# Fusion attention written out: key rows loaded, one maximum and one exponential over 1500 keys

## The reference

```
memory_proj = einsum('bme,de->bmd', memory, W_mem)
scores = einsum('bnd,bmd->bnm', hidden_states, memory_proj) / sqrt(256)
attn = softmax(scores, axis=-1)
memory_context = einsum('bnm,bmd->bnd', attn, memory_proj)
gate = sigmoid(concat([hidden_states, memory_context]) @ W_gate.T + b_gate)
fused = hidden_states + gate * memory_context; return rmsnorm(fused, norm_w)
```

## Time and profile before

| | |
|---|---|
| median of 3 runs | 1597.53 us (1596.61 to 1602.24) |
| the profiled execution | 1597.96 us, its span 1596.2 us |
| PE busy | 1476.0 us, 92% |
| DVE busy | 945.8 us, 59% |
| ACT busy | 621.8 us, 39% |
| POOL busy | 539.6 us, 34% |
| DMA moved | 82.96 MB, mean 52 GB/s |
| the stage in question | about 690.8 to 818.7 us |

### The profile page before, as it was taken

The page is one execution under the profiler, slowest core; times in us unless marked ns, Lnnn a source line. Parts: engine busy times, 40 slices in busy tenths (PEclk is TensorE's granted clock), DMA queues, the critical chain, the costliest instruction groups (busy, mean ns, idle before and its releaser), DMA issues.

```text
span 1596.2 us, 21925 instructions
## 1 busy us (share of the span) xinstructions
PE 1476.0 (92%) x8042; PEld 781.9 (49%) x8043; DVE 945.8 (59%) x1605; ACT 621.8 (39%) x1014; POOL 539.6 (34%) x425
## 2 busy tenths in 40 slices
PE   6779999999999899989988899999999889999898
PEld 3346555555555444446654344455344344555344
DVE  6877666666666264114437677777333768778440
ACT  1253466666666520035542233334122333333131
POOL 1620488888888910000001133332000133333000
PEclk9989999999999999989999999999999989999999
DMA  7001532232331140023212001110031001110000
GB/s 253 0 2 36 136 97 71 76 98 64 84 80 50 27 138 0 0 78 106 88 34 64 0 25 43 40 36 1 2 112 65 0 21 40 36 36 13 2 0 23
DMA packets 42276, 82.96 MB, mean 52 GB/s; under 512 B 6252, under 2 KB 28188, under 8 KB 42156
## 3 DMA queue, kind: packets, MB, share of 16 engines
q1 hardware_dynamic: 42160, 81.48, 17.7%
HBM read 59.31 MB, written 0.97 MB: 38 GB/s over the span
## 4 chain that ended last, share of the span: by engine, by line
PE 79%; DVE 12%; POOL 3%; ACT 2%; issue 2%; DMA 0%; SPq 0%; POOLq 0%; ACTq 0%; DVEq 0%
PE psum L1810 21%; PE psum L2393 8%; PE psum L2051 5%; PE psum L2027 5%; PE psum L2001 3%; PE psum L2334 3%; DVE WBZ L1713 3%; PE psum L1984 3%; PE psum L2201 3%; PE psum L1970 2%; POOL XN L780 2%; PE psum L2365 2%; DVE WA L1453 2%; PE psum L2401 2%; PE psum L2385 2%
## 5 line engine op out<-in xcount | busy, mean ns | idle before, releaser
L1453 DVE TENSOR_REDUCE WA<-psum 112x2 f32<-112x1000 f32 x192 | 229.8, 1201 | 89.9 <-PE psum L2001 89.9
L780 POOL TENSOR_TENSOR XN<-XN,WBZ 125x896 f32<-125x896 f32 x128 | 266.5, 2082 | 16.8 <-POOL XN L780 0.9
L1172 ACT ACTIVATE WA<-psum,y_bias 125x448 f32<-125x448 f32 x192 | 121.1, 633 | 227.7 <-PE psum L2388 226.7
L1006 ACT ACTIVATE WBZ<-psum 125x896 f32<-125x896 f32 x192 | 175.5, 915 | 43.9 <-PE psum L2027 33.3
L2393 PE MATMUL psum<-WA,ctxN 125*128 125x448 f32 x384 | 179.8, 552 | 0.4 <-ACT WA L1172 0.4
L812 POOL TENSOR_TENSOR XN<-const,y_max 112x896 bf16<-112x896 f32 x32 | 53.7, 1679 | 309.6 <-DVE y_max L1700 237.4
L1700 DVE CUSTOM_DVE_ANT_0 XA<-psum,WA 112x375 bf16<-112x375 f32 x240 | 122.7, 540 | 35.9 <-PE psum L2365 35.9
L803 POOL TENSOR_SCALAR ctxT<-ctxT 128x375 f32<-128x375 f32 x32 | 56.1, 1754 | 190.3 <-ACT std L881 187.8
L2027 PE MATMUL psum<-R 100*125 100x224 f16 x768 | 110.6, 266 | 0.0
L1713 DVE RECIPROCAL WBZ<-WBZ 128x224 f32<-128x224 f32 x68 | 105.2, 1549 | 1.2
L2365 PE MATMUL psum<-XB,R 128*112 128x375 f16 x240 | 77.7, 344 | 22.7 <-DVE y_max L1700 22.7
(11 more groups left out here) (266 smaller groups left out, 2567.4 us busy)
## 6 DMA issues: line engine op xcount, KB each, us to landing
R<-WA SPq DMA_DIRECT2D x192, 93.8 KB, 2.2
ctxT<-in_ctxT SPq DMA_DIRECT2D x12, 750.0 KB, 4.2
R<-in_ctxT SPq DMA_DIRECT2D x12, 750.0 KB, 5.4
WA<-in_ctxT SPq DMA_DIRECT2D x8, 750.0 KB, 4.2
ctxT<-in_ctxT SPq DMA_DIRECT2D x32, 187.5 KB
ctxN<-in_ctx SPq DMA_DIRECT2D x32, 187.5 KB
WBZ<-in_x_w SPq DMA_DIRECT2D x4, 1024.0 KB, 6.3
WA<-bias_rows SPq DMA_DIRECT2D x30, 82.0 KB, 3.8
```

What stands on the lines that cost most here:

```text
L780: nc.gpsimd.tensor_tensor(z_sum[b % 2][0:TK, :], first[0:TK, :], z_p[t % 4][0:TK, :], ALU.add)\
L1006: nc.scalar.activation(z_p[t % 4][0:TK, :].rearrange("p (k n) -> p k n", k=2), psum[0:TK, s:s + 2, 0:2 * GC], ACT.Exp, scale=float(CHD0) * ...
L1172: nc.scalar.activation(y_pT[t][0:TK, g * HALF:(g + 1) * HALF], bank[2 + u % 3][0:TK, 0:HALF], ACT.Exp, bias=y_bias[0:TK, bass.ds(b * NT + ...
L1453: V.tensor_reduce(z_mx[0:PR, r:r + 3:2, c], psum[0:PR, lo:lo + 2, 0:PC], AX_X, ALU.max)\
```

## The change

The stage is written out for all eight walks, without loops, and in another way:

- Key rows are loaded from in_ctx, two loads a walk of 125 partitions x 4 pieces of 1536 bytes (750 KB each). PE turns no context, and ACT copies none. Walk 0's rows are loaded with its columns; SP issues the rows of walk i when the values of walk i - 2 are done (m_pv), the columns when the scores of walk i - 2 are (m_scores). Both stand in SP's one list.
- The scores of a walk fill four banks (8 products). One maximum on DVE and one exponential on ACT read all 1500 columns. There is one set of four banks: scores of walk i + 1 wait for the exponential of walk i.
- The 12 probability parts are 125 adjacent columns each, turned four at a time, copied by ACT in three copies of 512 columns, and all 12 value products add up in one bank.
- The quotient is taken by DVE (m_divide) straight from that bank. The queries are read in place from XA, 64 columns each (8 of them belong to the next batch; their results are dropped).
- POOL has no part in the stage.

On SP:

```diff
-            with sp.Fori(0, HB // 2 - 1) as i:
-                for p in range(2):
-                    wait_alone(sp, "x1_scores", CHUNKS * (2 * i + p + 1) + 1)
-                    two_contexts(2 * i + p + 2, p)
+            def m_columns(i):
+                for j in range(2):
+                    b = 2 * i + j
+                    load(m_ctxT[i % 2][j], a["ctxT"][:, b * NK:(b + 1) * NK], f"m_columns{i % 2}")
+            def m_rows(i):
+                for j in range(2):
+                    at = (2 * i + j) * CHUNKS * TK
+                    load(m_ctxN[i % 2][j][0:TK].rearrange("k (c t) x -> k c (t x)", c=CHUNKS),
+                         a["ctx"][at:at + CHUNKS * TK, :].rearrange("(c k) x -> k c x", c=CHUNKS), f"m_rows{i % 2}")
...
+            m_columns(0)
+            m_rows(0)
             emptied(sp, ("down", 1, 1))
+            m_columns(1)
+            m_rows(1)
+            for i in range(2, HB):
+                sp.wait_ge(sem("m_scores"), i - 1)
+                m_columns(i)
+                sp.wait_ge(sem("m_pv"), i - 1)
+                m_rows(i)
+            sp.wait_ge(sem("m_pv"), HB)
```

On ACT (its m_turned copies four turned parts, its m_back the result turned back):

```diff
+            def m_exps(i):
+                act.wait_ge(sem("m_max"), i + 1)
+                if i > 1:
+                    act.wait_ge(sem("m_turned"), PARTS3 * (i - 1))
+                nc.scalar.activation(m_p[i % 2].rearrange("p (c k) -> p c k", c=CHUNKS), m_scores, ACT.Exp,
+                                     bias=nmax_all[:, i % 2:i % 2 + 1], accum_out=lsum_all[:, i % 2:i % 2 + 1])\
+                    .then_inc(sem("m_exp"), 1)
...
+            for i in range(HB):
+                m_turned(i, 0)
+                m_turned(i, 1)
+                if i + 1 < HB:
+                    m_exps(i + 1)
+                m_turned(i, 2)
+                if i > 0:
+                    m_back(i - 1)
```

On DVE:

```diff
+            def m_maximum(i):
+                dve.wait_ge(sem("m_scores"), i + 1)
+                if i > 1:
+                    dve.wait_ge(sem("m_exp"), i - 1)
+                V.tensor_reduce(nmax_all[:, i % 2:i % 2 + 1], m_scores, AX_XY, ALU.max, negate=True)\
+                    .then_inc(sem("m_max"), 1)
```

On PE (m_turned turns four parts of 125 columns, m_attended multiplies them with the key rows, m_back turns the result back):

```diff
+            def m_scored(i):
+                pe.wait_ge(sem(f"m_columns{i % 2}"), 32 * (i // 2 + 1))
+                if i > 0:
+                    pe.wait_ge(sem("m_exp"), i)
+                for u in range(CHUNKS):
+                    for j in range(2):
+                        at = i * PR + j * S
+                        mm = pe.matmul(bank[u][QP * j:QP * (j + 1), 0:CK], m_flat[:, at:at + QP],
+                                       m_ctxT[i % 2][j][:, u * CK:(u + 1) * CK], start=True, stop=True)
+                mm.then_inc(sem("m_scores"), 1)
...
+            m_scored(0)
+            for i in range(HB):
+                if i + 1 < HB:
+                    m_scored(i + 1)
+                m_turned(i, 0)
+                m_turned(i, 1)
+                if i > 0:
+                    m_back(i - 1)
+                m_attended(i, 0)
+                m_turned(i, 2)
+                m_attended(i, 1)
+                m_attended(i, 2)
```

More of the change, by code:

```diff
@@ L60 @@
 NT = NK // TK
+PARTS3 = NT // 4
 QG = 4
@@ L293, in build @@
                       .rearrange("p (b h s) -> p b h s", b=B, h=4) for t in (XB, XN))
-        cmax, nnew, ddec, alpha, rsum = (sb(n, [P, 4]) for n in ("cmax", "nnew", "ddec", "alpha", "rsum"))
+        cmax = sb("cmax", [P, 4])
         QH = HEADS * S
@@ L393, in take @@
             return bank[bk]
-        FOURS = 2 * NT // 4
         LANDED = 16 * 2
[L400 to L403, removed]
         def entry(eng, col, hi, lo=0):
             return eng.value_load(table[0:1, bass.ds(col, 1)], min_val=lo, max_val=hi)
[L408 to L449, removed]
         def ahead(b, t):
@@ L1589, in _, with m_divide @@
                     add_to_x(("down", h, m), m, h)
-            attention("x1", 0, None)
+            def m_maximum(i):
[4 more added lines that the diff above has]
+                    .then_inc(sem("m_max"), 1)
+            def m_divide(i):
+                dve.wait_ge(sem("m_exp"), i + 1)
+                if i > 1:
+                    dve.wait_ge(sem("m_normed"), i - 1)
+                then(V.reciprocal(rl[i % 2][:, 0:1], lsum_all[:, i % 2:i % 2 + 1]))
+                dve.wait_ge(sem("m_pv"), i + 1)
+                if i > 1:
+                    dve.wait_ge(sem("m_back"), i - 1)
+                V.tensor_scalar(m_o[i % 2], bank[6 + i % 2][:, 0:C], rl[i % 2][:, 0:1], None, ALU.mult)\
+                    .then_inc(sem("m_normed"), 1)
+            m_maximum(0)
+            for i in range(HB):
+                if i > 0:
+                    m_divide(i - 1)
+                if i + 1 < HB:
+                    m_maximum(i + 1)
+            m_divide(HB - 1)
             for h in range(2):
@@ new lines, in m_turned, with m_attended @@
+            def m_turned(i, g):
+                if g == 0:
+                    pe.wait_ge(sem("m_exp"), i + 1)
+                n = PARTS3 * i + g
+                if n > 1:
+                    pe.wait_ge(sem("m_pT"), n - 1)
+                for k in range(4):
+                    t = 4 * g + k
+                    mm = pe.transpose(bank[4 + n % 2][0:TK, k * P:(k + 1) * P], m_p[i % 2][:, t * TK:(t + 1) * TK], ident)
+                mm.then_inc(sem("m_turned"), 1)
+            def m_attended(i, g):
+                if g == 0:
+                    pe.wait_ge(sem(f"m_rows{i % 2}"), 32 * (i // 2 + 1))
+                    if i > 1:
+                        pe.wait_ge(sem("m_kept"), i - 1)
+                pe.wait_ge(sem("m_pT"), PARTS3 * i + g + 1)
+                for t in range(4 * g, 4 * g + 4):
+                    for j in range(2):
+                        q = slice(QP * j, QP * (j + 1))
+                        mm = pe.matmul(bank[6 + i % 2][q, 0:C], m_pT[i % 2][0:TK, t, q], m_ctxN[i % 2][j][0:TK, t, :],
+                                       start=(t == 0), stop=(t == NT - 1))
+                if g == PARTS3 - 1:
+                    mm.then_inc(sem("m_pv"), 1)
@@ new lines, in m_back @@
+            def m_back(i):
+                pe.wait_ge(sem("m_normed"), i + 1)
+                mm = pe.transpose(bank[6 + i % 2][:, C:2 * C], m_o[i % 2], ident)
+                mm.then_inc(sem("m_back"), 1)
+            m_scored(0)
+            for i in range(HB):
+                if i + 1 < HB:
+                    m_scored(i + 1)
+                m_turned(i, 0)
+                m_turned(i, 1)
+                if i > 0:
+                    m_back(i - 1)
[3 more added lines that the diff above has]
+                m_attended(i, 2)
```

299 lines of the change are left out of this document (22 added, 277 removed).

## The result

| | before | after |
|---|---|---|
| median | 1599.23 us (4 runs, 1596.61 to 1602.24) | 1618.58 us (4 runs, 1614.36 to 1619.24) |
| profiled execution | 1597.96 us, span 1596.2 | 1619.24 us, span 1617.5 |
| stage, its first product to the first product of mc | 691.11 to 818.71 = 127.6 us | 693.84 to 841.47 = 147.6 us |
| DMA moved by the queue | 81.48 MB | 93.77 MB |

The ratio is 1.011 (95% interval 1.0088 to 1.0132): slower by 1.1%, where 1593 us was forecast. Nearly all of it lies in the stage, which took 20.0 us more. The stage's first product is the first turning of the context before (its first scores follow at 701.36) and the first scores after. So stages are compared from their own first product.

What follows compares the result with a forecast made beforehand. Before, TensorE bounds the stage; after, loads on five engines, 16.4 us a walk. Next stage starts at 810.1 instead of 818.7; less 1 + 1 for clock and 2 for contention, about 5 us saved: 1593 us, range 1585 to 1610.

Steps and rivals of the forecast that it cites:

- TensorE's work and the chain: Fusion stage, per walk: TensorE needs about 7.2 us, the chain of waits 7.9 us, bounds 7.2 to 9.4.
- the end of the stage: Last walk's close: multiply 0.35, transpose and handovers 0.6, copy 0.26, together 1.2 us where it took 2.2 before.
- Five engines: Key-row loads: 125 partitions go to five of sixteen engines, so a pair takes 12.7 us instead of 3.66.
- The 75% of peak: Key-row loads: by this rule both pairs take about 9.4 us a walk; 1552 us, sharing the sixteen-engine rival's 7%.
- 16.4 us of loads a walk: Busiest five engines: 12.7 us of key rows plus 3.66 of key columns per walk, making loads the bound.
- Contention, "0 to 7 us in all; I take 2": Five engines slowed while eleven stream columns: 1.1 us a walk, 0 to 7 us in all, 2 taken.
- The rival of slow pieces: Key-row pieces 192,000 bytes apart in DRAM slow each engine: 1606 to 1631 us, chance 20%.
- Its threshold, 1.8 us a walk: Extra load time from which slow key-row pieces decide: 14.5 us a pair, 106 GB/s.
- The clock: TensorE waits some 8 us a walk, runs partly at 1.2 GHz; covered by loads except 1 + 1 us at the end.
- The rival of sixteen engines: All sixteen engines carry the key rows: 52 us saved, 1546 us, chance 7%.

Runs made afterwards that it cites:

- e2: Changed kernel without the key-row loads of walks 2 to 7 (values use old rows): 1562.57 us, one run.
- e12: Changed kernel with key rows in loads of 128 partitions of overlapping rows, and next walk's columns issued ahead of the rows: 1537.92 us, ratio to before 0.963.
- e1: Changed kernel with each key-row load of 125 partitions issued as two, of 112 and 13: 1561.75 us, ratio to before 0.972.
- e4: Changed kernel with the key-column loads of walks 2 to 7 written to DRAM instead of SBUF: 1589.72 us, one run.
- e3: Changed kernel where SP waits until the previous walk's key rows have landed before issuing key columns: 1608.86 us, one run.
- e11: Changed kernel with key-row loads of 128 partitions of other rows, in the same 1536-byte pieces, order of issue unchanged: 1554.28 us, one run.
- e13: Changed kernel with key rows in loads of 128 partitions of overlapping rows, values right, order of issue unchanged: 1556.23 us, one run.
- e14: Changed kernel with key-row loads of walks 2 to 7 bringing only 120 of 125 partitions, in one load: 1576.05 us, one run.
- e15: Changed kernel with key rows as 128 partitions of other rows, in two loads of 64 partitions: 1567.79 us, one run.
- e8: Kernel before the change, with context and probabilities turned in parts of 125 adjacent columns instead of every third: 1588.06 us, ratio 0.987.

## Why the prediction was wrong

The step that failed is one term of the sum: what it costs when key rows and key columns move at the same time. By its own steps:

- **TensorE's work and the chain: right.** 7.9 us was predicted for a walk that waits for no load; e2 and e12 measured 7.57. The maximum was put at 1.72 us (1.720), the exponential at 1.50 + 0.1 (1.513 + 0.20), the end of the stage at 1.2 (840.38 to 841.47, 1.1).
- **Five engines: right.** The share of 0.33 at 120 GB/s came as read from the earlier trace rows, and e1 took 53 us off the stage by splitting the loads. The 75% of peak that the Trainium skill, "DMA: Bandwidth & Descriptors", section "Bandwidth", gives for transfers of a megabyte and more was no fair rival: a load here is 750 KB, and the figures beside that rule are for 128 partitions. A pair of row loads, 1.5 MB, moved at 120 GB/s.
- **16.4 us of loads a walk: right where nothing meets.** e4 measured 16.3 to 16.9.
- **Contention, "0 to 7 us in all; I take 2": this step failed.** From the first data of walk 1's columns to the last key rows the prediction had 115.9 us (688.6 to 804.5); the changed kernel took 142.0 (691.5 to 833.5), 26 us more, where 2 stood. In the steady part, five walks took 102.87 us (716.04 to 818.91), 20.6 each, 4.2 more than 16.4. The prediction took its price from the later chunk loads in the earlier trace rows, 274 GB/s at a share of 1.10, charged it to the five engines only, and only for the 3.66 us that columns take alone. That gave 1.1 us a walk, 7 in all, and it took 2 of them without a reason; with all 7 it would have said about 1598, still short. The runs show that both sides slow down, to about half, so the overlap itself grows to some 6 us (741 to 747) and the five engines lose about 3 us of it; their own part of the columns comes behind that. e3 gives the bound from the other side: one after the other costs 19.0 us, with 2 of idle time in it.
- **The row was there.** A share of 1.10 with 274 GB/s in the earlier trace rows, next to 1.01 with 420 in the earlier trace rows, already said that a busy engine may move two thirds of its rate. It was read as the price of small pieces. e11 shows small pieces without that price. In the packet records of the earlier trace rows a 1536-byte piece takes 98 ns in the loaded slice and 65 in the later stretch, so the mixture of the 125-partition load with others, as here, is the likelier reason; no run took that stretch apart.
- **The rival of slow pieces** (1606 to 1631 us) holds the measured time, and its sign, walks of 18 us and more, came too, but not for its reason: four runs per partition, far apart in DRAM, cost nothing (65 ns and 120 GB/s when rows move alone). Its threshold, 1.8 us a walk, was passed by contention. A reader who went by the sign alone would have blamed the wrong cause.
- **The clock** fell as expected (0.70 in the steady part), and while loads were the bound it didn't matter. From the last key rows to the next stage 5.6 us were predicted at full clock, with 1 more for the clock; 8.0 were measured, at 0.63 of it.
- **The rival of sixteen engines** (1546 us) was not this kernel. Where the rows do go to sixteen engines at full rate, with the order of issue unchanged, the runs took 1554.28 and 1556.23 us (e11, e13); with the columns issued early e12 took 1537.92.

## What to carry to other kernels

Before a load replaces work on an engine, count the partitions of the load: with 125 instead of 128 the key rows moved at 120 GB/s instead of 384 to 402, and reading three rows too many gave the rate back. A DMA share near 1 doesn't mean that the loads run at full rate; put the GB/s of the same slice beside it, and where a share of 1 moves half of what it moves elsewhere, ask which partitions are being written at the same time. Loads that write SBUF side by side can take longer than the same loads one after the other.

## What the runs showed of the hardware

- Loads that write SBUF at the same time can slow each other down to about half: 65 to 125 ns and 229 to about 400 ns for a load of 125 partitions beside columns. Not when one of them writes DRAM (e4), nor when every load covers 128 partitions (e11 to e13).
- A load by itself can be as slow. One of 120 partitions, or two of 64, takes 124 ns a piece with nearly nothing beside it, where one of 128 takes 65 (e14, e15, e11).
- A turned tile that reads every third float32 column costs 258 ns of weight load, one of adjacent columns 187 (e8).
- SP is held while it issues: 7.65 us for a load of rows at 745.88 and 7.06 us for the two next column loads in the changed kernel. In e11 a load of rows at 750.21 held it for 0.51 us. That it waits for room in the queue is a guess; no run tested it. What stands behind in SP's list is late by that time: in the chain above, the columns at 739.61 follow 5.74 us of issuing.

```profile
745.88 7.65 SPq L470 DMA_DIRECT2D R<-in_ctx  x1
753.57 7.06 SPq L470 DMA_DIRECT2D R<-in_ctxT  x2
```
